# Work of the mixtures moved between engines: ScalarE makes the normalisations, the token scalings and E3T, GpSimd the update with Z

## The reference, cut to what matters

```python
x = x + tanh(g_xattn[0]) * L0_xattn(layernorm(x), ctx, ctx, ...)
x = x + tanh(g_ffn[0])   * L0_ffn(layernorm(x), ...)
x = x + tanh(g_xattn[1]) * L1_xattn(layernorm(x), ctx, ...)   # "matching"
x = x + tanh(g_ffn[1])   * L1_ffn(layernorm(x), ...)
# L0_ffn(X): X = X + self_attention(rmsnorm(X, norm1_w))      # this is Z
#            h2 = rmsnorm(X, norm2_w); logits = h2 @ router_w # 8 experts, 2 taken
#            return X + swiglu(h2, shared) + sum_e w_e * expert_e(h2)
# L1_xattn(hc, hq): w1, w2, w3 = split(w_sim)
#            Sim = (hc@w1)[:, :, None] + (hq@w2)[:, None, :] + (hc*w3) @ hq.T + b
#            A = softmax(Sim); B = softmax(max(Sim)); the rest: A@hq, B@hc, one product with W_qv
# L1_ffn(x): 16 experts of 64, 2 taken, and a shared one
```

## Time and profile before

| | |
|---|---|
| median of 3 runs | 529.53 us (529.13 to 532.28) |
| the profiled execution | 529.87 us, span 528.1 us from first to last instruction |
| PE busy | 465.9 us, 88% of the span |
| DVE busy | 379.5 us, 72% |
| POOL busy | 311.0 us, 59% |
| ACT busy | 268.6 us, 51% |
| mean granted TensorE clock | 0.96 of full speed |

### The profile page before, as it was taken

One profiled execution on the slowest core, in us unless ns is written; L12 is line 12 of the kernel. 1 busy time (PEld: TensorE's weight loads), 2 busy tenths in 40 slices (PEclk: granted clock), 3 DMA queues, 4 the chain that ended last, 5 costly groups with the idle time before them and its releaser, 6 DMA issues.

```text
span 528.1 us, 10878 instructions
## 1 busy us (share of the span) xinstructions
PE 465.9 (88%) x3679; PEld 347.3 (66%) x3702; DVE 379.5 (72%) x960; ACT 268.6 (51%) x505; POOL 311.0 (59%) x509
## 2 busy tenths in 40 slices
PE   3768869999999689869998989899989997988895
PEld 2646546777667468657776867587757765766673
DVE  5463647889998587987775788668976797667753
ACT  2231347777777456445457335644465447433452
POOL 6866787888964065526753466347635663354453
PEclk9996769999999899989999999999999999898999
DMA  6510000301001002000000000000000000000000
GB/s 161 135 63 0 2 1 2 113 2 53 3 11 45 2 1 51 1 0 1 1 1 1 2 0 2 0 0 0 0 0 2 0 1 20 2 1 21 0 20 22
DMA packets 19339, 9.81 MB, mean 19 GB/s; under 512 B 6520, under 2 KB 18777, under 8 KB 19289
## 3 DMA queue, kind: packets, MB, share of 16 engines
q1 hardware_dynamic: 17848, 8.84, 6.1%
q10 hardware_dynamic: 1440, 0.33, 0.3%
HBM read 8.12 MB, written 1.05 MB: 17 GB/s over the span
## 4 chain that ended last, share of the span: by engine, by line
PE 54%; DVE 19%; POOL 10%; issue 9%; ACT 4%; DMA 2%; SPq 1%; POOLq 0%; another core or an unknown queue 0%; DVEq 0%; ACTq 0%
PE PS L1746 9%; PE PS L1747 8%; PE PS L1748 8%; POOL HLO L583 4%; PE PS L1611 3%; PE PS L1617 3%; DVE work L1297 3%; PE PS L1606 3%; PE PS L1579 2%; PE PS L1651 2%; DMA X<-in_x_dram 2%; POOL grstd L600 2%; PE PS L1594 2%; DVE work L1302 1%; PE PS L1801 1%
## 5 line engine op out<-in xcount | busy, mean ns | idle before, releaser
L583 POOL TENSOR_TENSOR HLO<-work,HHI 128x512 fp32r<-128x512 f32 x112 | 144.7, 1294 | 139.4 <-ACT HHI L803 135.7
L810 ACT ACTIVATE work<-PS 128x512 f32<-128x512 f32 x112 | 66.9, 597 | 100.0 <-PE PS L1748 96.3
L1297 DVE TENSOR_TENSOR work<-work,PS 128x512 f32<-128x512 f32 x104 | 70.9, 682 | 50.2 <-ACT work L810 19.9
L803 ACT ACTIVATE HHI<-work 128x512 fp32r<-128x512 f32 x111 | 69.8, 629 | 42.2 <-DVE work L1302 42.1
L1302 DVE TENSOR_TENSOR work<-PS,work 128x512 f32<-128x512 f32 x112 | 77.1, 691 | 15.2 <-POOL HLO L583 6.2
L1022 DVE TENSOR_REDUCE nmax<-PS 128x4 f32<-128x512 f32 x64 | 42.3, 682 | 7.9 <-PE PS L1579 7.6
L697 ACT ACTIVATE EX<-PS 128x512 f32<-128x512 f32 x64 | 34.9, 605 | 13.5 <-PE PS L1594 13.4
L1746 PE MATMUL PS<-HHI,W0H_down 128*128 128x512 f32 x72 | 34.9, 485 | 0.2
L1746 PE MATMUL PS<-H2H,W0H_gate 128*128 128x512 f32 (+1 forms) x72 | 32.3, 449 | 1.5 <-issue 0.8
L1746 PE MATMUL PS<-H2H,W0H_up 128*128 128x512 f32 (+1 forms) x72 | 29.7, 412 | 2.9 <-DVE work L1302 2.9
L1747 PE MATMUL PS<-H2L,W0H_up 128*128 128x512 f32 (+1 forms) x72 | 28.6, 398 | 0.0
(11 more groups left out here) (355 smaller groups left out, 1210.4 us busy)
## 6 DMA issues: line engine op xcount, KB each, us to landing
X<-in_x_dram SPq DMA_DIRECT2D x4, 256.0 KB, 8.1
raw<-in_L_ffn_e_gate_dram SPq DMA_DIRECT2D x1, 1024.0 KB, 5.5
raw<-in_L_ffn_e_up_dram SPq DMA_DIRECT2D x1, 1024.0 KB, 7.7
out_dram<-X SPq DMA_DIRECT2D x4, 256.0 KB, 2.3
ctx_nat<-in_ctx_dram SPq DMA_DIRECT2D x2, 308.0 KB
raw<-in_L_ffn_We_gate_dram SPq DMA_DIRECT2D x1, 512.0 KB, 3.8
raw<-in_L_ffn_We_up_dram SPq DMA_DIRECT2D x1, 512.0 KB, 3.8
raw<-in_L_ffn_We_down_dram SPq DMA_DIRECT2D x1, 512.0 KB, 4.1
```

The costliest lines, as they stand in the source:

```text
L583: pool.tensor_tensor(HLO[t][:], HH[k % 2][:], HHI[t][:].bitcast(F32), ALU.subtract).then_inc(m_sem["lo"], 1)
L803: act.activation(HHI[turn_of(m, g, k)][:], HH[k % 2][:], ACT.Copy).then_inc(S["hi"], 1)
L810: act.activation(SG[c % 2][:], PS[:, c % 2, :], ACT.Silu).then_inc(S["silu"], 1)
L1297: dve.tensor_tensor(SG[c % 2][:], SG[c % 2][:], PS[:, 4, :], ALU.mult).then_inc(S["scaled"], 1)
```

## The change

Three moves. (1) `scaled_tokens` goes from DVE to ACT, with group 0 one slot later in the attention, and g = 1, 2, 3 in chunks 0, 2, 5. (2) `xn`, `hn` and `e3` go from DVE to ACT; `hn` now stands one chunk later except for the last group, and `e3` reads PSUM itself and stands ahead of `xt`. (3) `ffn_input` goes from DVE to POOL in pieces of two batches: a product into E3T, a wait, a sum, a wait. Four pieces stand between `low_tokens(0, 0)` and `token_scales(3 * GB, GB)` at the end of the attention, four in chunks 11 to 14 of group 0.

```diff
@@ POOL @@
+            def ffn_input(b):
+                pool.wait_ge(b_sem["zs"], b + 2)
+                at = E3T[:, 0:2 * D].rearrange("p (b d) -> p b d", b=2)
+                step(pool.tensor_scalar(at, Z[:, b:b + 2, :], tg[:, 2:3], None, ALU.mult))
+                step(pool.tensor_tensor(X[:, b:b + 2, :], X[:, b:b + 2, :], at, ALU.add))
+                if b % GB == 2:
+                    pool.sem_inc(m_sem["yx"], 1)
             token_scales(GB, 2 * GB)
             low_tokens(0, 0)
+            for b in range(0, 2 * GB, 2):
+                ffn_input(b)
             token_scales(3 * GB, GB)
...
+            mixtures(pool, chunks, by_chunk(..., *((11 + k, lambda k=k: ffn_input(2 * GB + 2 * k)) for k in range(4))), matching)
@@ ACT @@
+            def scaled_tokens(g):
+                if g == 0:
+                    act.wait_ge(r_sem[0]["root"], 2)
+                else:
+                    act.wait_ge(r_sem[0]["scale"], 3 if g == G - 1 else 2)
+                if g >= 2:
+                    act.wait_ge(r_sem[0]["t"], g)
+                for j in range(GB):
+                    b = g * GB + j
+                    ins = act.activation(HG[0][g % 2][:, j, :], Z[:, b, :], ACT.Copy, scale=rstd[:, b:b + 1])
+                ins.then_inc(r_sem[0]["h"], 1)
...
+                if of(0) == 10:
+                    scaled_tokens(0)
...
+                def normalised(dst, k, signal):
+                    for j in range(GB):
+                        ins = act.activation(dst[:, j, :], X[:, g * GB + j, :], ACT.Identity, bias=gnmr[:, k + j:k + j + 1],
+                                             scale=grstd[:, k + j:k + j + 1])
+                    ins.then_inc(signal, 1)
+                def xn():
+                    act.wait_ge(c_sem["hc"], g + 1)
+                    act.wait_ge(c_sem["sc"], g + 2)
+                    normalised(XG, 0, c_sem["xn"])
+                def hn():
+                    act.wait_ge(c_sem["sc"], g + 3)
+                    normalised(HG1, GB, r_sem[1]["h"])
+                def e3():
+                    act.wait_ge(c_sem["t"], g + 2)
+                    act.wait_ge(c_sem["s"], g + 1)
+                    act.wait_ge(c_sem["o"], g + 1)
+                    act.activation(E3T[:], PS[:, 7, :], ACT.Identity, bias=w2s[:], scale=w3s[:]).then_inc(c_sem["e3"], 1)
                 def xt():
-                    act.wait_ge(c_sem["t"], g + 2)
-                    act.wait_ge(c_sem["o"], g + 1)
                     act.activation(XGT[:], PS[:, 7, :], ACT.Copy).then_inc(c_sem["xt"], 1)
...
-                return by_chunk((9, xt), (13, exps), ...
+                return by_chunk((7, xn), (9, e3), (9, xt), (22 if is_last(g) else 26, hn), (13, exps), ...
...
+                                           (0, lambda: scaled_tokens(1)), (2, lambda: scaled_tokens(2)), (5, lambda: scaled_tokens(3)),
@@ DVE: scaled_tokens, ffn_input, norm_group, xn, e3 and hn are gone @@
-                if of(0) == 9:
-                    scaled_tokens(0)
+                if of(0) == 8:
+                    dve.sem_inc(R0["root"], 1)
...
-                                           (0, lambda: scaled_tokens(1)), (1, lambda: scaled_tokens(2)), (4, lambda: scaled_tokens(3)),
...
-                                           *((c, lambda g=g: ffn_input(g)) for g, c in enumerate((8, 15, 16, 17)))), matching)
```

More of the change, by code:

```diff
@@ L216, in build @@
                                             "t32", "v", "k_sb", "max", "m", "rden", "ct", "z", "zs", "xn", "split_k", "split_q")}
-        r_sem = [stage(f"r{m}", pe="t lg ct", act="ht ct_sb", dve="h e1 e2 cs" + " lg_sb top" * (m == 0), pool="low" + " scale" * (m == 0))
+        r_sem = [stage(f"r{m}", pe="t lg ct", act="h ht ct_sb", dve="e1 e2 cs" + " lg_sb top root" * (m == 0), pool="low" + " scale" * (m == 0))
                  for m in range(2)]
         r_chain = [sem(f"r{m}_chain") for m in range(2)]
-        m_sem = stage("m", pe="bc g u down yn", act="silu hi yt", dve="scaled hid yx x st", pool="lo")
-        c_sem = stage("c", pe="t s bt at bbt hq hc o", act="xt exp bexp at_sb hq_sb",
-                      dve="xn e3 mx a bb bc hcr xh wb xu x mv", pool="cg xb sc")
+        m_sem = stage("m", pe="bc g u down yn", act="silu hi yt", dve="scaled hid x st", pool="lo yx")
+        c_sem = stage("c", pe="t s bt at bbt hq hc o", act="xn e3 xt exp bexp at_sb hq_sb",
+                      dve="mx a bb bc hcr xh wb xu x mv", pool="cg xb sc")
         c_chain = sem("c_chain")
@@ L620, in matching @@
                                 (10, lambda: bias(2)), *of_end, (23 if is_last(g) else 27, lambda: low_tokens(1, g)))
-            mixtures(pool, chunks, by_chunk((2, lambda: low_tokens(0, 1)), (5, lambda: low_tokens(0, 2)), (8, lambda: low_tokens(0, 3))), matching)
+            mixtures(pool, chunks, by_chunk((2, lambda: low_tokens(0, 1)), (5, lambda: low_tokens(0, 2)), (8, lambda: low_tokens(0, 3)), *((11 + k, lambda k=k: ffn_input(2 * GB + 2 * k)) for k in range(4))), matching)
             rest(1, G, G * NCH[1] + OFF[1][0], -1)
@@ L865, in matching @@
                 r = (23, 25, 28) if is_last(g) else (27, 30, 34)
-                return by_chunk((9, xt), (13, exps), (13, bexp), (16, at_sb), (17, hq_sb), (r[0], lambda: turned_tokens(1, g)),
+                return by_chunk((7, xn), (9, e3), (9, xt), (22 if is_last(g) else 26, hn), (13, exps), (13, bexp), (16, at_sb), (17, hq_sb), (r[0], lambda: turned_tokens(1, g)),
                                 (r[1], rtanh), (r[2], ct_sb))
             mixtures(act, chunks, by_chunk(*((c, turn(t)) for t, c in enumerate(TURN_AT)), (0, lambda: turned_weights(0, 4, 0, GB)),
+                                           (0, lambda: scaled_tokens(1)), (2, lambda: scaled_tokens(2)), (5, lambda: scaled_tokens(3)),
                                            (1, lambda: turned_tokens(0, 1)), (4, lambda: turned_tokens(0, 2)), (7, lambda: turned_tokens(0, 3)),
@@ L1093, in better_root @@
                 lnc(dve.scalar_tensor_tensor(out=ROOT, in0=tb, scalar=1.5, in1=ROOT, op0=ALU.add, op1=ALU.mult))
[L1095 to L1103, removed]
             C0 = Chain(r_chain[0], 18)
@@ L1306, in chunks @@
                         f()
[L1308 to L1312, removed]
             def residual(m, g):
@@ L1343, in matching @@
             def matching(g):
[L1344 to L1348, removed]
                 def norm(i=g):
@@ L1357, in norm @@
                     ins.then_inc(c_sem["mv"], 1)
[L1359 to L1368, removed]
                 def mx():
@@ L1419, in update @@
                     ins.then_inc(c_sem["x"], 1)
-                def hn():
-                    dve.wait_ge(c_sem["sc"], g + 3)
-                    norm_group(HG1, GB, r_sem[1]["h"])
                 def route_a():
@@ L1431, in matching @@
                 s = (18, 20) if is_last(g) else (19, 21)
-                steps = [(5, norm), (7, xn), (9, e3), (11, mx), (12, bmax), (14, soft), (17, bcol), (18, product),
+                steps = [(5, norm), (11, mx), (12, bmax), (14, soft), (17, bcol), (18, product),
                          (s[0], weights), (s[1], update)]
@@ L1435, in matching @@
                     steps += [(21, lambda: norm(G))]
-                r = (22, 24, 24, 25, 25, 26) if is_last(g) else (25, 28, 29, 30, 31, 32)
-                steps += [(r[0], hn), (r[1], route_a), (r[2], lambda: two_largest(1, CR, GB)), (r[3], lambda: places_of_two(1, CR, GB)),
-                          (r[4], lambda: (weights_of_two(g, CR), weighted_places(1, CR, GB))), (r[5], lambda: in_pieces(1, g, CR, GB))]
+                r = (24, 24, 25, 25, 26) if is_last(g) else (28, 29, 30, 31, 32)
+                steps += [(r[0], route_a), (r[1], lambda: two_largest(1, CR, GB)), (r[2], lambda: places_of_two(1, CR, GB)),
+                          (r[3], lambda: (weights_of_two(g, CR), weighted_places(1, CR, GB))), (r[4], lambda: in_pieces(1, g, CR, GB))]
                 return by_chunk(*steps)
@@ L1442, in _ @@
             mixtures(dve, chunks, by_chunk(*((c, turn(t)) for t, c in enumerate(TURN_AT[:9])),
-                                           (0, lambda: scaled_tokens(1)), (1, lambda: scaled_tokens(2)), (4, lambda: scaled_tokens(3)),
                                            (3, lambda: logits_of_group(1)), (6, lambda: logits_of_group(2)), (9, lambda: logits_of_group(3)),
                                            (9, lambda: less_largest(1)), (10, lambda: places(1)), (11, lambda: difference_of_two(1)),
-                                           (13, lambda: weights_in_place(1)), (14, lambda: weights_in_pieces(1)),
-                                           *((c, lambda g=g: ffn_input(g)) for g, c in enumerate((8, 15, 16, 17)))), matching)
+                                           (13, lambda: weights_in_place(1)), (14, lambda: weights_in_pieces(1))), matching)
             residual(1, G)
```

## The result

| | before | after |
|---|---|---|
| median of 9 runs each | 529.13 us (526.64 to 533.07) | 532.38 us (530.41 to 538.74) |
| ratio after / before | | 1.0061, 95% interval 1.0034 to 1.0088 |
| busy DVE / ACT / POOL | 379.5 / 268.6 / 311.0 us | 353.0 / 286.3 / 323.2 us |

What follows compares the result with a forecast made beforehand. PE was taken as the fullest engine (88%), so a faster DVE is worth only PE's waits for it. Terms -0.7 + 0.9 - 1.4 - 0.8 + 4.0 + 1.7 = +3.7 gave 533.2 us, range 525.5 to 538.5.

Steps and rivals of the forecast that it cites:

- Duration of ACT's four: Four ACT normalisation instructions in a row take 1.5 us, bounds 1.1 and 2.0, against DVE's 3.05.
- Group 1, -0.7: xn alone in group 1: PE's 0.88 us wait goes, late hid(8) gives some 0.2 back; -0.7 us.
- Groups 2, 3 and layer 1, +0.3 each: xn and hn together on ACT: hn 0.9 us later, XG's turn saves about 0.6; +0.3 each, +0.9 for three.
- the second rival: ACT late for hn: four take 2.0 us, lower clock behind three waits of about 2; 537 us, chance 0.22.
- Last group, -1.4: hn alone in the last group: 1.5 us instead of 3.05, PE's 3.58 wait falls to about 2.1; -1.4 us.
- scaled_tokens, -0.8: Group 1's scaled tokens on ACT ready before PE needs them: 0.96 us wait goes, 0.2 for late silu; -0.8 us.
- E3T, nothing: e3 costs ACT about 0.8 us more in chunk 9, hidden by PE's chunk 10; no effect.
- Pieces, +4.0 and +1.7: POOL's ffn_input pieces hold up DVE instructions: +4.0 us in group 0's chunks 10 to 14, +1.7 at the attention's end.
- The first rival: The pieces are free, DVE's instructions falling in POOL's gaps: 527.5 us, about 525 with faster ACT; chance 0.27.
- The third: Rival: Identity not in silu's table, two loads of 1.283 us at each of 12 places; over 548 us, chance 0.03.
- the fourth: Rival: DVE's relief halves PE's 6.5 us of waits at the scaling L1297; 530 us, chance 0.08.

Runs made afterwards that it cites:

- after's second: Second profiled execution of the changed kernel, nothing altered, taken because the first profile was of the longest of nine runs; 530.85 us.
- the kernel with XG alone: Kernel before with only XG's four normalisations (xn) moved to ACT, in chunk 7; 520.96 us beside 529.98, ratio 0.9804.

## Why the prediction was right, and where only its total was

The total was 3.7 us over before; the ratios say 3.2 (1.8 to 4.7), and the traces 4.1: 3.4 in the mixtures and 0.7 of PE's longer wait at the end of the attention. (The two profiled executions as a whole are only 1.0 us apart, since before lost more to the clock ahead of the mixtures.) Its terms, one by one:

- **Duration of ACT's four.** Taken at 1.5 us, measured 1.65 (four of about 0.483 that overlap). The Trainium skill's estimate of 1.64 (ScalarE: Activation LUTs, What ACT_TABLE_LOAD costs) was the better one.
- **Group 1, -0.7.** Measured -0.71. PE's wait for XG is gone, and chunk 10 gives 0.35 back.
- **Groups 2, 3 and layer 1, +0.3 each.** The order on ACT was read rightly: XG, silu, rounding, HG. The waits came out at 2.20, 2.21 and 1.81 where the working gave 1.85 (0.95 and 0.9 more). At full clock that is +0.5 for groups 2 and 3, and +0.2 to 0.3 for layer 1. But behind such a wait the clock falls more often than not, and then the place costs 2.1. This was the second rival, "the lower clock behind three waits of about 2", of which only the clock came true, not the 2.0 us for four that stood beside it. For groups 2 and 3 it was the truer case: the term should have been about +1.7 each, the mean over the eight places. In layer 1 the clock fell in none of the four traces.
- **Last group, -1.4.** There was no gain. Five traces have this wait; the group came out within -0.1 to +0.2 in three and at +1.0 and +1.1 in two, after's second among them, in which the granted clock over the 5 us behind the wait was 0.50 and not 0.66. The failing step is "nothing is ahead of `hn` but the factors". What stands behind it was looked at only as far as silu(3). The YT copy of `out_t` is queued there too, and down(0) on PE needs it ahead of HG. Moved behind the copy, the gain came: -1.3, close to the forecast.
- **scaled_tokens, -0.8.** Measured -1.18: the wait of 0.96 and its pipeline break, with nothing given back in chunks 2 and 5. ACT's four took 1.27 there.
- **E3T, nothing.** No difference was seen: 520.74 us with it on ACT, 521.42 on DVE.
- **Pieces, +4.0 and +1.7.** Measured +1.0 and +0.67 with the pieces alone. (In after's traces the end of group 0 costs 1.2; 0.2 of it is also there without the pieces.) They were counted as one DVE instruction held per POOL instruction. The five of `weights_in_place(1)` were set at 3.45 against 1.1, but in before they took 2.35, for the wait behind L583 was already among them; that alone is 1.25 of the error. The other part is that POOL's one-input product hardly holds DVE: 0.49 and 0.42 instead of the 0.7 that the product was taken for. At the end of the attention one DVE instruction was held, by 0.5, and not two and a half by 0.7. The rule of the Trainium skill that was cited against this part (SBUF — State Buffer, Who interferes with whom) has the instruction that comes second wait for the whole of the first. The runs agree for POOL's two-input sums and not for its product, as far as the profiled ends of POOL's instructions go.

So the forecast was right on the total by luck, because two errors met: the pieces were 4 us too dear, and the last group and the clock together about as much too cheap. The first rival (pieces free) and the second (ACT late) were each half true, on opposite sides. The third did not come, ACT has ten table loads in both kernels; nor did the fourth, PE's waits for L1297 went from 6.5 to 6.8.

What neither the sum nor a rival had is the largest effect of all. XG and HG wait for the same factors, and DVE made them one after the other. Split over two engines they gain 1.5 to 1.8 us in three places and 5.5 in all, and the runs were 7 to 9 us faster with what the clock did. The change moved both to ACT, and so kept them in a row, with a silu and a rounding between them. The same row without the two between it gained 1.0 to 1.2 us in each of the three places (HG, XG in chunk 8), so the two between them cost more than the row itself.

## What to carry to other kernels

When jobs are moved off a busy engine, look which of them start at the same signal and give them to different engines. If they stay in a row, keep other work from between them: moved with a silu and a rounding in the middle, the pair here only moved the wait. Before moving a job that waits, list everything behind it in the new queue to its end, copies of another step too, and put it behind what is ready earlier: one line in ACT's list was worth 7 us here. A wait of 2 us on PE is to be priced with what the clock does behind it, as a chance, not as a constant: here 1.6 us in 6 of 8 places.

## What the runs showed of the hardware that I had not expected

- Identical waits, with the same work ahead of them, are followed by a lower clock in one execution and not in the next. In group 3 after's first execution fell to 0.59 over 2 us, its second stayed at 1.00. And behind the wait of 2.65 to 2.70 us for L1331 in layer 1, group 1 (L1297 in before), the granted clock over the next 3.5 us was 0.50 to 0.70 in ten of thirteen traces, and 1.00 in three. That alone is 1.3 us, and it makes comparisons of single profiles uncertain by that much at each such place. Two rows (columns as the earlier trace rows), the first of before, the second of the kernel with XG alone:

```profile
449.50:452.40 2.90, 2.85 (x12) 2.15 (x13) 2.07 (x3) 1.11 (x2) 1.28 (x1) 0.50 0.00 0
```

```profile
443.20:444.80 1.60, 1.54 (x13) 1.20 (x13) 1.53 (x4) 0.81 (x2) 0.13 (x1) 1.00 0.00 0
```

- The same transposes and down matmuls take 2.9 us in the first and 1.6 in the second.
- A DVE instruction with two SBUF inputs beside a POOL TENSOR_SCALAR of 0.93 us takes 0.42 to 0.49 us (0.26 alone), beside a POOL TENSOR_TENSOR it takes all of what is left of that one: 0.68 beside a sum of 0.75, 1.33 beside one of 1.29.
